# Opening of an AdaLN, attention and FFN kernel: five constant products left out, demodulation products moved between the first high products, one table load moved

## The reference

```python
def _L0_cond_ref(x, w, weight, bias, affine_w, affine_b):
    styles = w @ (affine_w * gain).T + affine_b
    ws = weight[None, :, :] * styles[:, None, :]
    dcoefs = jax.lax.rsqrt(jnp.sum(ws * ws, axis=2) + 1e-08)
    xm = x * styles[:, None, :]
    y = jnp.einsum('blc,oc->blo', xm, weight)
    y = y * dcoefs[:, None, :]
    y = jnp.clip(y + bias, -CLAMP, CLAMP)
```

## Time and profile before

| what | value |
|---|---|
| median of three executions | 1724.02 us |
| profiled execution | 1723.94 us |
| its span | 1722.0 us |
| TensorE matmul busy | 1710.7 us |
| TensorE weight loads busy | 1385.7 us |
| VectorE, ScalarE, GpSimd busy | 1248.9, 881.5, 728.8 us |

### The profile page before, as it was taken

One profiled execution on the slowest core, in us unless ns is written; L12 is line 12 of the kernel. 1 busy time (PEld: TensorE's weight loads), 2 busy tenths in 40 slices (PEclk: granted clock), 3 DMA queues, 4 the chain that ended last, 5 costly groups with the idle time before them and its releaser, 6 DMA issues. The chain is left out here.

```text
span 1722.0 us, 23035 instructions
## 1 busy us (share of the span) xinstructions
PE 1710.7 (99%) x7748; PEld 1385.7 (80%) x7756; DVE 1248.9 (73%) x1842; ACT 881.5 (51%) x1306; POOL 728.8 (42%) x642
## 2 busy tenths in 40 slices
PE   9999999999999999999999999999999999999998
PEld 7888888888888888888888888778787787787776
DVE  7766776658989688687464434457997988888876
ACT  7656556556666576575553222233554444543533
POOL 1122221222677465656571000005656755855823
PEclk9999999999999999999999999999999999999999
DMA  6011101120233434232445666887635444535411
GB/s 211 1 49 50 49 0 48 49 74 25 98 123 106 163 99 147 88 119 88 171 147 195 203 212 211 318 298 259 224 113 157 114 140 146 154 103 163 135 43 61
DMA packets 119959, 221.94 MB, mean 129 GB/s; under 512 B 25442, under 2 KB 25890, under 8 KB 119860
## 3 DMA queue, kind: packets, MB, share of 16 engines
q1 hardware_dynamic: 94308, 161.99, 27.8%
q10 hardware_dynamic: 18384, 33.56, 6.1%
q0 software_dynamic: 7168, 25.17, 4.9%
HBM read 158.26 MB, written 58.75 MB: 126 GB/s over the span
## 5 line engine op out<-in xcount | busy, mean ns | idle before, releaser
L1088 PE MATMUL bank<-h_parts,mlp_w 128*128 128x512 f32 x2016 | 459.3, 389 | 0.6 <-ACT product_copy L1308 0.5
L1088 PEld LDWEIGHTS bank<-h_parts,mlp_w 128*128 128x128 f32 x2016 | 378.1, 188 | 80.4 <-ACT product_copy L1308 1.4
L352 PE MATMUL bank<-h_parts,gate_w 128*128 128x512 f32 x1536 | 351.1, 389 | 0.6 <-DVE h_parts L702 0.5
L352 PEld LDWEIGHTS bank<-h_parts,gate_w 128*128 128x128 f32 x1536 | 288.1, 188 | 61.9 <-issue 0.9
L2167 PE MATMUL bank<-operand_parts,int_w 128*128 128x512 f32 x1152 | 274.9, 394 | 0.1
L1153 PE MATMUL bank<-p_parts,mlp_out_w 128*128 128x512 f32 x1152 | 267.4, 391 | 0.0
L2167 PEld LDWEIGHTS bank<-operand_parts,int_w 128*128 128x128 f32 x1152 | 213.7, 188 | 49.4 <-issue 4.8
L1153 PEld LDWEIGHTS bank<-p_parts,mlp_out_w 128*128 128x128 f32 x1152 | 214.7, 188 | 48.0 <-issue 3.4
L1429 POOL TENSOR_TENSOR product_out<-product_out,gelu 128x512 f32<-128x512 f32 x69 | 119.7, 1756 | 95.7 <-DVE product_out L1588 95.1
L627 POOL TENSOR_TENSOR decay_sq<-decay 128x512 f32<-128x512 f32 x32 | 39.2, 1226 | 278.8 <-DVE decay L715 278.8
L1308 ACT ACTIVATE product_copy<-bank,vec_sb 128x512 f32<-128x512 f32 x144 | 99.1, 688 | 107.0 <-PE bank L1088 105.8
(11 more groups left out here) (322 smaller groups left out, 2733.9 us busy)
## 6 DMA issues: line engine op xcount, KB each, us to landing
p_tile<-p_d ACTq DMA_DIRECT2D x96, 256.0 KB, 4.9
p_d<-product_out SPq DMA_DIRECT2D x92, 256.0 KB, 2.0
raw_mlp_w<-mlp_gate_g SPq DMA_DIRECT2D x21, 512.0 KB, 3.7
raw_mlp_w<-mlp_fc_g SPq DMA_DIRECT2D x21, 512.0 KB, 4.2
xin<-xT SPq DMA_DIRECT2D x8, 1024.0 KB, 6.8
hs_d<-u SPq DMA_DIRECT2D x8, 1024.0 KB, 5.0
hs_pair<-hs_d SPq DMA_DIRECT2D x8, 1024.0 KB, 7.4
x_columns<-xT SPq DMA_DIRECT2D x8, 1024.0 KB, 6.9
```

The source lines that it names most:

```text
L352: i = pe.matmul(bank[:], gw[:, w, s, k, m * P:(m + 1) * P], hr[:, q, t, k, :], start=k == 0 and n == 0, stop=k == KT - 1 and n == 2)
L1088: i = pe.matmul(bank[:], wb[g % 2][:, s, w, kk, :], hop[u % 2][o][:, t, kk, :], start=first and kk == 0 and n == 0, stop=kk == 1 and n == ...
```

## The change

```diff
             def project_first_high():
-                narrow = [(m, k) for m in (2, 3) for k in range(KT)]
+                narrow = [(m, k) for m in range(1, KT) for k in range(KT)]
                 for k in range(KT):
                     pe.wait_ge(w_high, k + 1)
                     pe.wait_ge(x_high, k + 1)
                     for m in range(KT):
                         pe.matmul(YB[0][m][:], cw[:, 0, k, m * P:(m + 1) * P], XP[0][:, 0, k, :], start=k == 0, stop=False)
-                        if (KT * k + m) % 3 < 2 and narrow:
+                        if m < KT - 1:
                             demodulation(*narrow.pop(0))
 
             def prepare():
...
                         i = pe.matmul(I[0][:, 2 * m:2 * m + 2], aff[:, k, m * P:(m + 1) * P],
                                       condT[:, 2 * k:2 * k + 2], start=k == 0, stop=k == 1)
-                    if m < KT - 1:
-                        keep_clock(1)
                 i.then_inc(s_sty_ps, 1)
                 keep_clock(3)
                 pe.wait_ge(s_wsq, 2)
                 pe.wait_ge(s_dch, 7)
                 pe.wait_ge(s_sty2, 1)
-                for m in range(2):
-                    for k in range(KT):
-                        demodulation(m, k)
-                        if k % 2:
-                            keep_clock(1)
+                for k in range(KT):
+                    demodulation(0, k)
+                    if k % 2:
+                        keep_clock(1)
                 project_first_high()
...
                 split_high(0)
+                act.activation(small[:, 62:63], quarter, ACT.Sqrt)
                 x_early(0)
                 split_high(1)
                 split_high(2)
-                act.activation(small[:, 62:63], quarter, ACT.Sqrt)
                 act.wait_ge(s_dem, 1)
```

## The result

The changed kernel took 1729.90 us in the median of ten executions, 1723.66 to 1731.51, against 1724.02 us before, 1723.39 to 1724.80. The ratio is 1.0029, with a 95% interval from 1.0021 to 1.0037: it became slower. The ten executions are not spread evenly. Two took 1723.66 and 1724.41 us, eight took 1729.45 to 1731.51 us. The profiled one is of the second kind: 1730.88 us, span 1729.0 us.

The account below looks back on a forecast made before the run. TensorE bounds the kernel, busy 1710.7 of 1722.0 us. The opening's terms sum to 0.68 us: 1723.94 - 0.68 = 1723.26 us, forecast as a 1723.3 us median, range 1722.1 to 1724.9 us.

Parts of the forecast that it names:

- The clock: Rival: TensorE's clock falls in the sixteen style weight loads, costing about 2.14 us, 1725.4 us; chance 0.08, twice or more 0.02.
- Parts 1 to 4: Opening up to the first low product: fewer constant products, a 0.44 us wait for x; low products start 0.68 us earlier.
- my bound: If removing the constant products between the style products gave nothing: first low product at 19.08 us, 0.44 us earlier.
- Part 1: Style products: three constant products go, so the style and its square come 0.68 us earlier; four loads cost 0.52 us.
- Part 5: Last demodulation product starts 0.25 us later; first y tile then waits for the demodulation, near 21.4 us, costing nothing.
- Part 6: ScalarE's table load, moved ahead of the wait for x: hidden there at no cost, 1.5 us without that wait.
- Part 7: Behind the first low product: later work and waits hang on TensorE's chain, so the 0.68 us carries through.

Follow-up runs that it names:

- Both back: Changed kernel with three constant products put back between the style products and one after each of four demodulation products ahead of the high ones: 1724.00 us.
- run 1: Changed kernel with the three constant products between the style products put back: 1723.50 us, ratio 0.9996.
- run 7: Kernel before with only the one-element square root and its table load moved ahead of the wait for x: 1723.77 us, ratio 1.0001.
- Run 2: Changed kernel with a constant product after each of four demodulation products ahead of the high ones: nine at 1722.67 to 1724.31 us, two at 1731.70 and 1731.89.
- run 4: Changed kernel with its twelve demodulation products behind the sixteen high products instead of between them: 1724.93 us.
- run 5: The changed kernel itself measured again, nothing altered: 1729.58 us, ratio 1.0024 against the kernel before.
- Run 9: Changed kernel without any constant product behind 8 us, twelve demodulation products still between the high ones: 1732.35 us.
- run 10: Changed kernel without any constant product behind 8 us, all sixteen demodulation products ahead of the high ones: 1727.33 us.
- run 3: Kernel before with only the three constant products between the style products removed: nine held, median 1723.37 us; three fell, 1728.82, 1730.26 and 1731.52.
- run 8: Changed kernel with six instead of three constant products behind the style products: 1723.98 us, ratio 1.0000.

## Why the prediction was wrong

The clock fell, the rival that the prediction gave 0.08 and left out of its range. Of its steps, the sum of the parts held to some tenths of a us where the clock held, and the chance and the price of that rival failed.

**Parts 1 to 4, 0.68 us.** Shown by the runs that take single terms. Style constants out alone: first low product at 18.94 us, forecast for the change 18.84. Style constants back: 19.07 us against the 19.08 of my bound. Both back: 19.62 against 19.54. The starts of the style products differ by up to 0.3 us between these traces, so that is the accuracy of the agreement. Counted from the first style product, the first low one comes after 11.46 us before, 10.80 with the style constants out and 11.04 with them back, that is 0.66 and 0.42 us sooner (forecast 0.68 and 0.44). Part 1 took its 0.52 us for four loads from a demodulation row; the style rows have 0.64, which changed nothing in the sum. In the five executions in which the changed kernel's clock held it took 1722.62, 1722.86, 1723.41, 1723.66 and 1724.41 us; the three of the second group have spans 1.0 us shorter than the kernel before beside them, the two of the first (1721.6 and 1721.8) 0.2 to 0.4 us shorter than its profiled execution (1722.0). The wait for x that took back part of the gain was there, 0.78 us instead of 0.44.

**Part 5, the last demodulation product.** The first y tile was to wait for GpSimd instead of TensorE. In the changed kernel's trace this can't be seen, since all was late. In run 1 it can, in the timelines of its ScalarE and of its gates:

```profile
21.54 0.78 ACT L579 ACTIVATE y<-bank,vec_sb,small 128x512 f32<-128x512 f32 x1 [1.62 <-POOL small L640]
```

```profile
39.99 16.60 PE L352 MATMUL bank<-h_parts,gate_w 128*128 128x512 f32 x72 [0.55 <-DVE h_parts L701]
```

The tile is released by GpSimd's power, and the gates still start 0.44 us before the 40.43 us of the earlier trace rows, so in this kernel, where the demodulation products stand as in the changed one, their later end cost nothing on the path that shows.

**Part 6, the table load.** Right, by run 7. In the changed kernel too the square root started 1.30 us after the load (8.80 and 10.10), with no idle time between them that would be a drain.

**Part 7, what carries it on.** Right, but it carried the loss: 7.28 us at the gates, 7.0 at the end.

**The clock.** This is the step that failed, and in both its terms. First its chance: 0.08, where it fell in 17 of 22. I had argued that the gap is short and that idle times of 0.29 and 0.58 us had not brought the slow pace back. That looked at idle times. Run 2 fell without any beyond the 0.30 us that the kernel before has as well, so a fall needs no longer wait. Whether the changed kernel's wait for x (0.78 and 0.99 us in its two traces) makes it fall more often is open: it has fewer constant products and a longer wait at once. In the runs, by the constant products between the first style product and the first high product:

| kernel | constant products there | fell |
|---|---|---|
| before, also with the root moved | 10 | 0 of 111 (101 and 10) |
| both back | 10 | 0 of 11 |
| style constants back; six behind | 8 | 0 of 22; 0 of 11 |
| style constants out alone | 7 | 3 of 12 |
| wait filled | 7 | 2 of 11 |
| changed | 5 | 17 of 22 |
| behind the high products (run 4) | 5 | about 7 of 11, by the spans |
| none, mixed; none, ahead | 0 | 4 of 4; 10 of 10 |

Whatever their place, fewer of them went with more falls, within each of the three groups too. With two fewer than before it held, with three fewer it fell at times, and the change takes out five. Whether two fewer is safe or only rarer isn't settled: 33 executions can miss a chance of a few per cent.

Second its price: 2.14 us, read from the start of the kernel, where the clock came up under constant products alone. In the changed kernel it fell just ahead of the mixed stretch of high and demodulation products or just behind its first high product, and it stayed down through that stretch in all four traces in which it had fallen by then (the first trace, runs 2, 5 and 9); it came back 2.4 to 5.2 us into the low products. The slow stretch of the first trace lasted 17 us, not 4.6 (2.14 us of loss at 0.2 us a product are 10.7 products at 0.43 us), and cost 5.32 + 2.43 = 7.75 us. The 2.43 us in the low products are near the 2.14; what the prediction left out are the 5.32 us of the mixed stretch ahead of them. Run 9 against run 10 shows this by a change of order alone, 5.0 us apart: 8.3 us of loss with the mixture, 3.3 us with the demodulation ahead. This price was there before the change, by run 3. So it was the missing constant products that made the kernel slower. The four demodulation products that moved lengthened the mixed stretch from 24 to 28 products, and in run 1, where the clock held, they cost nothing. The Trainium skill's rule (TensorE: Matmul & The Clock Gate, What's actually happening), that the low clock is the default and activity releases it, was right in direction; the same section has the low clock come back after an idle time, and here it came with TensorE at work (run 2, between 11.6 and 12.3 us).

What stays open: why one execution of the same program falls and the next doesn't. The moment at which the clock comes up in the first microseconds varies from one execution to the next as well (the sixteen constant products took 5.07 us in one trace and 6.32 in another). A common cause of both is a guess that no run was made to show.

## What to carry to other kernels

Products that nobody reads can hold the clock, and whether they are needed is not seen in the trace in which they do their work: take them out one or two at a time, and run each step more than ten times, since a fall in one execution of five is missed by three executions half of the time. Look at spans and granted clocks too: in run 4 the times hide most of the falls. Price a fall by what follows it. If narrow products are mixed into the stretch behind, as here, the clock stays down until large ones come in a row, so put a dense stretch behind a thin one and not a mixed one. Filler in a wait is cheap but not free: with three constant products more (run 8) the median span was 1721.3 us, where the three held executions of the changed kernel beside it had 1720.6 to 1720.8.

## What was not expected of the hardware

- At the slow clock a demodulation product (two weight loads, 2 columns) took twice its time too: high and demodulation product together 0.855 us instead of 0.455.
- The clock rose under large products alone 2.4 to 5.2 us after they began (runs 2, 4, 5, 9 and 10, the changed kernel), and not in 11.7 us of large and 2-column products in turn.
- The granted clock reads 1.00 in the first microseconds, though products of 512 columns are 0.43 us apart there, which is 1.2 GHz; after the first fall it reads 0.50 where the pace says so. In these traces it isn't to be relied on before its first change.
